# A graph layer and a mixture of experts on one core: the set-up reordered, the stretch behind the last graph written out by engine, expert numbers loaded for sixteen tiles at once

## What is computed

```python
h = layernorm(x)
Xw = h @ Wv + bv
e = leaky_relu(sj[:, None, :] + si[:, :, None] + ab)      # sj, si = Xw times the two halves of aw
T = adj * exp(e); T = T / (T.sum(-1) + 1e-12)
H = h @ Wk[0] + bk[0] + (T @ h) @ Wk[1] + bk[1] + (T @ T @ h) @ Wk[2] + bk[2]
x = x + relu(H)

r = layernorm(x)
probs = softmax(r @ switch_w.T + switch_b); route = argmax(probs); p = max(probs)
pos = number of earlier rows with the same route
y = r @ expert_w[route].T + expert_b[route]               # r itself where pos >= 1228
x = x + y * p
```

## Time and profile before

| | us |
|---|---|
| median of three runs | 768.35 (768.01 to 769.15) |
| the profiled execution, its own time | 767.28 |
| its span, first to last instruction | 765.5 |
| PE busy | 711.6 (93%) |
| DVE busy | 647.9 (85%) |
| ACT busy | 480.2 (63%) |
| POOL busy | 444.1 (58%) |

### The profile page before, as it was taken

The page is one execution under the profiler, slowest core; times in us unless marked ns, Lnnn a source line. Parts: engine busy times, 40 slices in busy tenths (PEclk is TensorE's granted clock), DMA queues, the critical chain, the costliest instruction groups (busy, mean ns, idle before and its releaser), DMA issues.

```text
span 765.5 us, 18802 instructions
## 1 busy us (share of the span) xinstructions
PE 711.6 (93%) x4791; PEld 624.2 (82%) x4791; DVE 647.9 (85%) x3100; ACT 480.2 (63%) x1504; POOL 444.1 (58%) x523
## 2 busy tenths in 40 slices
PE   1899999999999999999999999999999999877783
PEld 1788888778888888898889899898889899756663
DVE  3799999999989999899989999999989988785552
ACT  1457777766666666666666666666666766654551
POOL 4224445546666666666656666666666665575563
PEclk9999999999999999999999999999999999979998
DMA  9423444433344444444443344444443323353430
GB/s 266 118 85 97 138 138 154 151 127 119 123 144 153 147 146 153 128 150 139 146 141 118 121 143 149 145 140 147 134 134 128 115 89 101 99 167 112 120 104 1
DMA packets 93035, 100.15 MB, mean 131 GB/s; under 512 B 10427, under 2 KB 85240, under 8 KB 92930
## 3 DMA queue, kind: packets, MB, share of 16 engines
q1 hardware_dynamic: 77860, 66.74, 30.1%
q0 software_dynamic: 13008, 30.07, 10.8%
q10 hardware_dynamic: 2064, 2.13, 1.1%
HBM read 49.92 MB, written 54.72 MB: 137 GB/s over the span
## 4 chain that ended last, share of the span: by engine, by line
PE 86%; DVE 6%; issue 3%; ACT 1%; SPq 1%; DMA 1%; POOL 1%; POOLq 0%; DVEq 0%; ACTq 0%
PE ps_z12a L1160 11%; PE ps_z12b L1160 11%; PE ps_lgb L1160 9%; PE ps_z0a L1160 9%; PE ps_z0b L1160 8%; PE ps_lga L1254 6%; PE ps_z0b L1261 4%; PE ps_z0a L1261 4%; PE ps_z12b L1220 4%; PE ps_xt L1194 3%; PE ps_xt L1188 3%; PE ps_z12a L1220 3%; PE ps_lgb L1290 3%; PE ps_t L1242 2%; PE ps_t L1211 2%
## 5 line engine op out<-in xcount | busy, mean ns | idle before, releaser
L524 POOL DMA_INDIRECT out<-lent,tok x143 | 145.8, 1020 | 151.3 <-DVE lent L1121 136.0
L507 POOL DMA_INDIRECT rowbuf<-rows,idx x128 | 129.8, 1014 | 55.0 <-issue 30.1
L572 ACT CAST xth<-ps_xt 128x256 fp32r<-128x256 f32 x128 | 47.8, 373 | 123.6 <-PE ps_xt L1194 123.3
L475 POOL TENSOR_SCALAR x<-xin,nm,r 128x256 f32<-128x256 f32 x128 | 85.1, 665 | 27.6 <-PE ps_xt L1194 19.3
L1254 PEld LDWEIGHTS ps_lga<-swc,xft 128*128 128x128 f32 x512 | 76.8, 191 | 14.2 <-ACT xft L575 3.4
L646 ACT ACTIVATE x<-rin 128x256 f32<-128x256 f32 x143 | 86.8, 608 | 1.7 <-DMA rin<-rowbuf 1.7
L471 POOL TENSOR_TENSOR r<-ve,mhalf 128x4 f32<-128x4 f32 x32 | 34.2, 1069 | 77.7 <-ACT ve L618 77.7
L588 ACT ACTIVATE od<-rows,oc,oa 128x256 f32<-128x256 f32 x128 | 77.0, 602 | 0.1
L753 DVE TENSOR_TENSOR xtl<-ps_xt,xth 128x256 fp32r<-128x256 f32 x128 | 54.0, 422 | 20.6 <-ACT xft L575 19.6
L1254 PE MATMUL ps_lga<-swc,xft 128*128 128x16 f32 x512 | 66.2, 243 | 2.9 <-ACT xft L575 2.9
L1194 PE MATMUL ps_xt<-ident,x 128*128 128x128 f32 x256 | 49.5, 275 | 9.4 <-POOL x L475 8.5
(11 more groups left out here) (205 smaller groups left out, 2358.8 us busy)
## 6 DMA issues: line engine op xcount, KB each, us to landing
rin<-rowbuf SPq DMA_DIRECT2D x143, 130.0 KB, 2.3
xin<-in_x SPq DMA_DIRECT2D x32, 512.0 KB, 4.0
out<-od SPq DMA_DIRECT2D x32, 512.0 KB, 5.4
ain<-in_adj SPq DMA_DIRECT2D x32, 256.0 KB, 4.6
ewr<-in_ewT SPq DMA_DIRECT2D x16, 256.0 KB, 2.9
out<-lent,tok POOLq DMA_INDIRECT x143, 3.0
rowbuf<-rin ACTq DMA_DIRECT2D x1, 2080.0 KB, 10.8
rowbuf<-rows,idx POOLq DMA_INDIRECT x128
```

The source lines that it names most:

```text
L475: pool.tensor_scalar(x0[:, g % 2, :], xin[:, g % BODY, :], nm1[:, q, g % G:g % G + 1], r1[:, q, g % G:g % G + 1], ALU.add, ALU.mult).then_ ...
L507: pool.indirect_dma_start(out=rowbuf, out_offset=bass.IndirectOffsetOnAxis(ap=idx[:, i:i + 1], axis=0), in_=rows[:, r, :], in_offset=None, ...
L524: pool.indirect_dma_start(out=out.rearrange("g n d -> (g n) d"), out_offset=bass.IndirectOffsetOnAxis(ap=tok[:, i % RY:i % RY + 1], axis=0 ...
```

## The change

**Set-up.** The raw weights of hops 1 and 2 (`w12r`) are loaded by two DMAs of 256 KB that ACT issues first, those of hop 0 by a third (`w0r`), behind an `Exp` of one column; SP no longer issues them. `bkr` moves behind the first two groups of `x` and `adj`. Waits are split: `d_w12`, `d_w0`, `d_bk`, `d_r` in place of `d_w`. DVE takes the statistics of graphs 0 to 3 first, then `bvb` and the remainders `w12l`, then the `xtl` of graph 0 (slot -1), then the attention columns with `w0l` (`attention_columns`), then the statistics of graphs 4 to 6, slot 0, the sum of the hop biases, slot 1. ACT makes `ve` and `nm` of the first four graphs ahead of `w12h`, which is now made in two halves. PE computes the product with `bvb` behind the first transposes. POOL runs a `pow` of its own before the tables' constants, and clears `ebp` in two halves, in slots 4 and 5. SP's loads of the split expert biases move into its loop, step 1.

**Behind the last graph.** The slots end at 128. What is left is written out for each engine: DVE interleaves the table step of batch 30 (tiles 104 to 107) with the routing of batch 31, tile by tile; then `last_step` for batch 31; `last_tiles` is cut into six turns that run behind the tiles 99 to 104. POOL scatters all rows that are left (119 to 127), then all tiles from 96 on. ACT spreads the default rows over the tiles. PE turns graph 126's rows in slot 128 already.

**The tiles of the tail.** PE runs `expert(i)`, then `turn(i + 2)`; ACT `high(i + 1)`, `norm(i + 2)`; DVE `low(i + 1)`, `finish(i)`. The numbers of the experts are loaded by one instruction for several tiles (`experts_of`): three at tile 97, four at 100, 104 and 108, sixteen at 112, fifteen at 128. A woven tile still has a load of its own, by the same function with one element.

```diff
 FIRST_STEP = 4
 LAG_TILE = 16
-REST = 2
...
-            sp.dma_start(bkr, bk.rearrange("(a k) d -> a k d", a=1).to_broadcast([P, 3, D])).then_inc(d_w, 16)
-            for kt in range(KT):
-                ks = slice(kt * P, (kt + 1) * P)
-                sp.dma_start(w12r[:, kt, 0:D], Wk[2, ks, :]).then_inc(d_w, 16)
-                sp.dma_start(w12r[:, kt, D:2 * D], Wk[1, ks, :]).then_inc(d_w, 16)
-                sp.dma_start(w0r[:, kt, 0:D], Wk[0, ks, :]).then_inc(d_w, 16)
             sp.dma_start(xin[:, G:2 * G, :], xd[1]).then_inc(d_x[1], 16)
             sp.dma_start(ain[:, 0:G, :], ad[0]).then_inc(d_a[0], 16)
-            sp.dma_start(swb[:], sb_.rearrange("(a o) -> a o", a=1).to_broadcast([P, E])).then_inc(d_w, 16)
-            sp.dma_start(sw[:], swT.rearrange("(t p) e -> p t e", p=P)).then_inc(d_w, 16)
+            sp.dma_start(swb[:], sb_.rearrange("(a o) -> a o", a=1).to_broadcast([P, E])).then_inc(d_r, 16)
+            sp.dma_start(sw[:], swT.rearrange("(t p) e -> p t e", p=P)).then_inc(d_r, 16)
             sp.dma_start(ain[:, G:2 * G, :], ad[1]).then_inc(d_a[1], 16)
+            sp.dma_start(bkr, bk.rearrange("(a k) d -> a k d", a=1).to_broadcast([P, 3, D])).then_inc(d_bk, 16)
             sp.dma_start(ebr[:], eb).then_inc(d_eb, 16)
-            load(2, 2)
             load_expert(0)
-            for q in range(3, NB):
+            for q in range(2, NB):
                 load(q, q)
             load_expert(1)
-            sp.wait_ge(s_eb, 2)
-            sp.dma_start(parts[0].bitcast(F32), ebh[:].bitcast(F32)).then_inc(d_ebp, 16)
-            sp.dma_start(parts[1].bitcast(F32), ebl[:].bitcast(F32)).then_inc(d_ebp, 16)
-            sp.wait_ge(d_ebp, 32)
-            sp.wait_ge(s_ebz, 1)
-            sp.dma_start(ebp[0:2, :].bitcast(F32), parts.rearrange("r e d -> r (e d)").bitcast(F32)).then_inc(d_ebp, 16)
+
+            def load_biases():
...
-                if 2 <= c < NG + 2:
+                if c == 1:
+                    load_biases()
+                if c >= 2:
                     store(c - 2)
...
+                if it * BODY + k in (4, 5):
+                    half = (it * BODY + k - 4) * E * D // 2
+                    pool.memset(ebp[:, half:half + E * D // 2].bitcast(F32), 0.0).then_inc(s_ebz, 1)
...
+            pool.tensor_tensor(first[:], onesf[:, 0:G], mhalf[:], ALU.pow)
...
             pool.wait_ge(s_pc, 12)
-            phase_a(pool, slot_fn, -LEAD_X0, LAG_OUT)
-
-
-            for i in range(WOVEN + LAG_OUT - REST - 2, NT):
+            phase_a(pool, slot_fn, -LEAD_X0, 1)
+
+            for g in range(OUT_LEFT - IT * BODY, G30):
+                row_scatter(IT, g)
+            tokens(IT, G30)
+            row_scatter(IT, G30)
+            row_factors(IT, G31)
+            for g in range(G30 + 1, G31):
+                row_scatter(IT, g)
+            tokens(IT, G31)
+            for g in range(G31, BODY):
+                row_scatter(IT, g)
+            for i in range(WOVEN - 1, NT):
                 scatter(i)
 
 
...
-            act.copy(w12h[:], w12r).then_inc(s_wh, 1)
+            w12d = [Wk[2].rearrange("(t p) d -> p t d", p=P), Wk[1].rearrange("(t p) d -> p t d", p=P)]
+            for h in range(2):
+                act.dma_start(w12r[:, :, h * D:(h + 1) * D], w12d[h]).then_inc(d_w12, 16)
+            act.wait_ge(s_pc, 2)
+            act.activation(e1[:, 0, 0:1], onesf[:, 0:1], ACT.Exp)
+            act.dma_start(w0r[:, :, 0:D], Wk[0].rearrange("(t p) d -> p t d", p=P)).then_inc(d_w0, 16)
 
             def slot_fn(it, k):
                 g = k + LEAD_XT
                 gx = k - LAG_XFT
...
+                    high(i + 1)
                 if i + 2 < NT:
-                    high(i + 2)
-                if i + 3 < NT:
-                    norm(i + 3)
-
-            phase_a(act, slot_fn, -LEAD_STATS, LAG_OUT)
-            for i in range(WOVEN + LAG_OUT - REST - 1, NT):
+                    norm(i + 2)
+
+            for k in range(-LEAD_STATS, G - LEAD_STATS + 1):
+                slot_fn(0, k)
+            act.wait_ge(d_w12, 32)
+            for kt in range(KT):
+                act.copy(w12h[:, kt, :], w12r[:, kt, :]).then_inc(s_wh, 1)
+            phase_a(act, slot_fn, G - LEAD_STATS + 1, 1)
+
+            turned_rows(IT, BODY - 2)
+            norm(WOVEN)
+            norm(WOVEN + 1)
+            turned_rows(IT, BODY - 1)
+            row_moments(IT, G31)
+            high(WOVEN)
+            default_rows(IT, OUT_LEFT - IT * BODY)
+            exponentials(IT, G31)
+            left = OUT_LEFT + 1
+            for i in range(WOVEN, NT):
                 tile(i)
+                for g in range(left, min(left + 2, B)):
+                    default_rows(IT, g - IT * BODY)
+                left += 2
 
 
         @block.vector
...
+            def remainders():
+
...
+            def attention_columns():
+
...
+            def hop_biases():
+
...
                 whole_tiles(c)
                 running(c)
                 limits(c)
                 advanced(c)
 
-            def last_tiles():
+            def last_tiles(turn):
...
                                          rin[:, r, 0:D], ALU.mult, ALU.add).then_inc(b_fin, 1)
 
             def tile(i):
-                if i + 2 < NT:
-                    low(i + 2)
+                if i + 1 < NT:
+                    low(i + 1)
                 finish(i)
 
...
             dve.wait_ge(s_pc, 12)
+            for k in range(-LEAD_STATS, -LEAD_STATS + G + 1):
+                slot_fn(0, k)
             dve.wait_ge(d_v, 16 * 4)
             for t in range(KT):
                 link(dve.tensor_scalar(bvb[:, t, :], onesf[:], bvt[:, t:t + 1], None, ALU.mult))
-
-            for k in range(-LEAD_STATS, -LEAD_STATS + G + 1):
+            remainders()
+            for k in range(-LEAD_STATS + G + 1, 0):
                 slot_fn(0, k)
-            set_up()
-            phase_a(dve, slot_fn, -LEAD_STATS + G + 1, LAG_OUT)
-
-            for i in range(WOVEN + LAG_OUT - REST - 1, NT):
+            attention_columns()
+            for g in range(G, LEAD_STATS):
+                input_stats(0, g)
+                if g < LEAD_STATS - 1:
+                    input_moments(0, g)
+            slot_fn(0, 0)
+            hop_biases()
+            phase_a(dve, slot_fn, 1, 1)
+
+            c = NG - 2
+            norm_field(IT, G30)
+            dropped(IT, G30)
+            default_factors(IT, G30)
+            row_of_token(IT, G30)
+            advanced(c - 1)
+            biased_sum(IT, BODY - 1)
+            residual(IT, BODY - 1)
+            row_stats(IT, BODY - 1)
+            row_moments(IT, BODY - 1)
+            finish(WOVEN - 1)
+            backlog(c)
+            whole_tiles(c)
+            running(c)
+            low(WOVEN)
+            starts(c)
+            passed(c)
+            scaled_logits(IT, G31)
+            rises(c)
+            add_bias(IT, G31)
+            steps(c)
+            top_logit(IT, G31)
+            picked(c)
+            differences(IT, G31)
+            tile_rows(c)
+            candidates(IT, G31)
+            tile_experts(c)
+            first_candidate(IT, G31)
+            reached(c)
+            limits(c)
+            one_hot(IT, G31)
+            advanced(c)
+            tile(WOVEN)
+            sum_probs(IT, G31)
+            probability(IT, G31)
+            positions(IT, G31)
+            own_positions(IT, G31)
+            own_rows(IT, G31)
+            norm_field(IT, G31)
+            dropped(IT, G31)
+            default_factors(IT, G31)
+            row_of_token(IT, G31)
+            tile(WOVEN + 1)
+            last_step(NG - 1)
+            for i in range(WOVEN + 2, NT):
                 tile(i)
+                if i < WOVEN + 8:
+                    last_tiles(i - WOVEN - 2)
 
 
         @block.tensor
...
+
+            def experts_of(i, m):
+                pe.wait_ge(s_tab, step_of(i))
+                _, at_i = nc.values_load_multi_w_load_instructions(
+                    tab_exp[0:1, i:i + m], [mybir.EngineType.PE], min_val=0, max_val=E - 1)
+                for j in range(m):
+                    at[i + j] = at_i[j]
 
             def expert(i):
                 if i == 0:
...
+                if i < WOVEN:
+                    experts_of(i, 1)
+                e = at.pop(i)
                 pe.wait_ge(b_lo, i + 1)
...
 
             def tile(i):
+                expert(i)
+                if i + 1 < STEPPED and (i + 1) % G == 0:
+                    experts_of(i + 1, G)
+                if i + 1 >= STEPPED and (i + 1 - STEPPED) % LOADED == 0:
+                    experts_of(i + 1, min(LOADED, NT - i - 1))
                 if i + 2 < NT:
                     turn(i + 2)
-                expert(i)
-
-            phase_a(pe, slot_fn, -LEAD_XT, LAG_OUT)
-            for i in range(WOVEN + LAG_OUT - REST - 1, NT):
+
+            slot_fn(0, -LEAD_XT)
+            pe.wait_ge(s_vc, KT)
+            for t in range(KT):
```

(15 more changed lines are left out.)

357 lines of the change are left out of this document (195 added, 162 removed).

## The result

The changed kernel takes 774.08 us (median of four runs, 772.96 to 775.19) where the kernel before, run beside it, takes 768.43 (768.01 to 769.15): a ratio of 1.0072, 95% interval 1.0055 to 1.009. It is 0.7% slower, where 749.6 was forecast. Its profiled execution takes 772.96 with a span of 771.2.

What follows compares the result with a forecast made beforehand. PE paces the slots, waiting chains the set-up, and a loop of latencies the steady tail. Set-up 6.2 plus tail 12.6 gives 18.8 us off the median 768.35, so 749.6 us, range 746.2 to 760.0.

Steps and rivals of the forecast that it cites:

- The set-up: Before the first slot: shorter chain turns the first exponential's input at 18.2 against 24.70; 6.2 us net, ends 4.9 and 7.3.
- Clearing `ebp` in two halves: POOL, slots 4 and 5: 1.76 us each, taken at nothing; shared SBUF interfaces could cost up to 1 or 2 us.
- The slow `pow`: POOL's set-up: the first `pow` takes 2.01 us against 1.04; running one early in spare time removes the slowness.
- The head: Start of the tail, to tile 105: PE's idling during the chain of last tables goes; 3.6 us gained, ends 0 and 5.
- what is late next is DVE itself: Head of the tail: once PE's idling goes, DVE without pauses sets the time; tile 105 ends at 691.8.
- The steady tile: Tiles 105 to 142: without the load's gap on PE, 1.38 us per tile for 1.644; 9.8 us over 37 tiles.
- The loop of ACT: Steady tail: transposes, `high`, `norm`, next transposes take 1.28 us plus 0.1 to reach PE, setting 1.38 per tile.
- Rival 1: Steady tail: PE's gap is address arithmetic, not the load; the rate stays 1.644, median 759.4; chance 0.18.
- The long loads: Steady tail: loads of sixteen and fifteen numbers taken at 0.4 us each, 0.8 together; bounds nothing and 10 us for both.
- Rival 2: Head of the tail: gains nothing, as PE's clock falls while it waits; median 753.2; chance 0.20.
- Rival 3: Slots: the 97 woven tiles' new load form shows 0.32 us gaps each, 31 us; median 780.6; chance 0.07.
- rival 4: Whole kernel: first half, set-up stays slow; second, long loads cost what the gap cost; within 1.5 us of 768.35; chance 0.03.

Runs made afterwards that it cites:

- group 3: Runs beside the kernel before on a chip without late signals; its table column is the changed kernel unaltered, run again: 764.24 us, ratio 0.9949.
- group 4: Runs on one chip with late signals: the changed kernel again, 774.00 us; the changed kernel without the scatters of tiles 96 to 107, 765.87 us (one run).
- ahead: Changed kernel, long loads without number checks, the kernel before's order inside a tile, ACT and DVE one tile further ahead: 749.25 us, ratio 0.9757.
- groups 1, 4 and 5: Sets of runs, each on one chip beside the kernel before, on two chips with late signals; the changed kernel there took 774.00 us.
- groups 2 and 3: Sets of runs, each on one chip beside the kernel before, on two chips without late signals; the changed kernel there took 764.24 us.
- after_again: The changed kernel unaltered, run again on a third chip: 764.24 us, ratio 0.9949 to the kernel before.
- each_unchecked: Changed kernel with a load for each tile, without the bounds check: 748.34 us (0.9751), 747.63 (0.9732), and 762.41 (0.9937) on a chip with late signals.
- group 2: Runs on one chip without late signals: three variants without load checks at 748.34 to 749.25 us, and one without twelve scatters at 761.75.
- one_each: Changed kernel with a checked load for each tile, as in the kernel before: 760.53 us (0.9909), and 756.28 (0.9845) on another chip.

## Why the prediction was wrong, point by point

The span of the profiled execution, cut at the forecast's own points. Slot 128's turning is L1346's last.

| stretch | before | forecast | the result | group 3 |
|---|---|---|---|---|
| start to first L1346 | 24.70 | 18.2 | 17.15 | 17.63 |
| to slot 128's L1346 | 632.96 | 0.3 more | 631.70 | 634.27 |
| to tile 105 | 37.25 | 33.65 | 40.73 | 33.64 |
| tiles 105 to 142 | 60.83 | 51.9 | 71.78 | 68.02 |
| tile 142 to the end | 9.7 | same | 9.8 | 9.7 |

**The set-up was right, and small by 1 us.** 7.6 against 6.5 us at the first L1346. The chain was the forecast one: L1346 waits for DVE's `svs`. The first `xin` landed at 5.66, where 5.9 was taken, though ACT's two loads ran beside it. The turn-taking of the DMA engines that the Trainium skill describes (DMA: Bandwidth & Descriptors, Queues, rings and completion order) would have put it later; the 4.9 us from issue to landing are inside the 4.0 to 6.1 of before, so this trace shows no cost of it. Clearing `ebp` in two halves was free: PE is busy 29.98 of 30 us in that stretch, and DVE 27.23, where it was 27.16. The slots themselves scatter by 2 us either way from run to run, 630.3 to 634.3 us, which no step of the forecast can meet.

**The slow `pow` was misread.** The `pow` that counts began at 8.82 and took 1.01, as forecast. But the early one, put there to be slow in its place, took 1.04 at 2.99, in this trace and in all eighteen others with the changed set-up. So the 2.01 us of before do not come from being the first. In before that `pow` starts inside an operation of DVE with two inputs in SBUF:

```profile
16.12 1.23 DVE L682 TENSOR_TENSOR w12l<-lent,w12h 128x1024 fp32r<-128x1024 f32 x1 [1.61 <-ACT w12h L562]
```

It ends 1.03 us behind that one's end at 17.35, as if it had waited for it. One trace shows this once, so the cause stays open; the early `pow` bought nothing that any trace shows.

**The head was right where PE's signals are in time.** 3.6 us were forecast and group 3 has 3.6 (37.25 to 33.64), with the last `row_of_token` at 669.72, where 675.8 - 6.2 = 669.6 was forecast, and DVE busy 9.55 of 10 us from 676 to 686. In the result it is 3.5 worse than before in place of 3.6 better, and of these 7.1 us the stall at tile 101 is 6.7: 8.66 us, against the 1.92 of group 3. The step that failed is "what is late next is DVE itself". The new order lets POOL issue its row scatters and those of the tiles in one go, and on a chip with late signals the stall comes with them: without twelve of the tiles' scatters it is gone (group 4). The forecast looked at POOL only for whether it would be in time, not for what it does to others.

**The steady tile: right mechanism, size off by 0.08.** The load with its check was what held PE before, and of the two mostly the check (group 3): without them the tile falls from 1.644 to 1.46 us (steady stretch of group 3: tiles 114 to 127, 18.79 us, 1.445 each). 1.38 was forecast. The loop of ACT is as described: turning at 748.16, `high` at 748.60, `norm` at 748.87, the next turning at 749.62, which is 1.46. From the turning to the end of `norm` it is 1.31 (1.28 was taken), and back to PE 0.15 (0.1). Over 37 tiles 3 us. Rival 1 (the gap is not the load) fell.

**The long loads: the step that failed on every chip.** 0.8 us were taken, and in group 3 they cost 7.49 + 7.86 - 2 x 1.46 = 12.4, in the result 6.87 + 7.06 - 2.9 = 11.0. The bounds were "at least nothing, at most sixteen times the 0.32 of one, 10 us", and I took the value nearest to the lower end because one instruction loads them. A row against it was in the trace of before, on the line of the load: three instructions of the sequencer, two of them a check. Whether the check comes once for each load or for each number that row could not say, and so the upper end could not be ruled out. It was the right one, and even short: PE stands for 5.33 us behind sixteen numbers, 0.33 for each, where the bound had 0.32. The clock fell in each stall, but how much of the price that is no run shows. For loads without checks, of which the forecast did not speak, 0.8 would have been near: in ahead both together cost 2.03 + 2.69 - 2.9 = 1.8 us.

**Late signals: not in the forecast at all.** Group 4 against group 3 of the same kernel: 774.0 - 764.2 = 9.8 us, 7.86 - 1.92 = 5.9 of it at tile 101 and 72.03 - 68.02 = 4.0 in the steady tail. Together: 749.6 + 11.6 (loads) + 3 (tile) - 1 (set-up) = 763, near the 764.2 of group 3, and 9.8 more give 773, near the 774.1 of the result. That ahead, without the checks and on a chip without late signals, comes out at 749.25 where 749.6 was forecast is in part luck: its steady tail takes 53.8 us for 51.9, and its set-up and slots together 1.9 less than forecast.

Rival 2 (the head gains nothing) was on the right side for another reason than it gave: what it names, the clock at half in the head, is there in group 3 as well (0.56 from 660 to 668, 0.50 from 668 to 676), and the head gains its 3.6 us all the same. Rival 3 (the loads of the woven tiles) fell: PE is full in the slots. Of rival 4 the first half fell, and the second was right and too mild: the long loads cost 11.6 us more than was taken, and the shorter tile gives back 37 x 0.184 = 6.8. The range, 746.2 to 760.0, had the loads' upper end of 10 us neither in the forecast's own range nor in a rival. With it the forecast alone gives 749.6 + 9.2 = 758.8, so the range stopped about where one bound of one term ended, and nothing was kept for two terms at their bad ends together.

**What stays open.** Why PE's signals are late. That it goes with the chip is seen in all groups: with them on two chips (groups 1, 4 and 5) and in the runs of the result, without on two (groups 2 and 3). Only the chip of groups 1 and 4 came up twice; on the others nothing separates the chip from whatever else differed from group to group. That POOL's scatters bring it on is shown by leaving them out, in the stall and in the steady tail, on the chips that have it, by one run each. How the one acts on the other, and why a signal comes 1 us late in one place and 7 in another, no run shows. The traces split in a second way that goes with it: with late signals they have records of 10,400 to 10,700 updates of semaphores, without 14,800 to 15,100, and the difference runs through the slots too. For the 143 signals of PE's turnings of tiles the trace of the result has 61 records, that of after_again 144. What that has to do with the lateness, and whether the recording has a part in it, no run shows. The trace of the kernel before is of the second kind (15,103), so that it has no late signal says nothing of the other chips. All that is known of it there is its time, 767.3 to 767.7 us in all five groups.

**The best version** is each_unchecked: the changed kernel with a load for each tile and without the check. 747.6 to 748.3 us on two chips (ratio 0.9732, interval 0.9707 to 0.9758, in group 3) and 762.4 on a chip with late signals (0.9937). ahead was within 1 us of it in group 2. On the chip with late signals one_each and the set-up alone were at 760.5 and 760.7 (761.05 the second time), not clearly apart from it.

## What to carry to other kernels

An instruction that replaces sixteen may still stand for sixteen times the work: look at the view of its own line for what the sequencer runs behind it (here two instructions, 0.285 us, for each number), and multiply those unless a row shows that they come once. Where a bound of a term is 10 us and the row for the chosen value is missing, the bound belongs into the range. And a reordering that lets one engine run without pauses is to be tried on more than one chip, beside the kernel before each time: here the same program was 0.5% faster on one chip and 0.9% slower on another.
